# A linear attention product moved next to the probabilities' product, and its query transposes put into the run of the other transposes

## The reference, cut to what matters

```
def causal_linear_attn(q, k, v):                 # BUCKET = 64, e = 32
    q = softmax(q, axis=-1);  k = elu(k) + 1.0
    bq, bk, bv = (z.reshape(b, h, n // BUCKET, BUCKET, e) for z in (q, k, v))
    k_cum = cumsum(bk.sum(axis=-2), axis=-2)
    ctx = cumsum(einsum('bhund,bhune->bhude', bk, bv), axis=2)
    ctx = ctx / (k_cum[..., None] + 1e-06)
    ctx = pad(ctx, one bucket in front)[:, :, :-1]
    return einsum('bhund,bhude->bhune', bq, ctx).reshape(b, h, n, e)

def local_attn(q, k, v):                         # window 128, looks one window back
    dots = where(causal or padding, -max, einsum(q, k2) * e ** -0.5)
    return einsum(softmax(dots), v2)

for i in range(DEPTH):                           # 4 layers, dim 256, 8 heads of 32
    x = x + self_attention(layer_norm(x), Wq, Wk, Wv, Wo, bo)   # local heads, then linear heads, @ Wo
    x = x + gelu(layer_norm(x) @ W1 + b1) @ W2 + b2
```

## Time and profile before

| | us |
|---|---|
| three executions | 957.61, 958.55, 958.65 |
| the profiled execution, its own time | 958.88 |
| its span, first to last instruction | 957.0 |
| PE busy / PEld busy | 944.3 (99%) / 815.4 |
| DVE / ACT / POOL busy | 672.8 (70%) / 612.4 (64%) / 480.0 (50%) |

### The profile page before, as it was taken

How to read it: one execution, slowest core, us unless ns; L and a number is a source line. 1 busy time by engine, 2 the same in 40 slices (tenths; PEclk the granted TensorE clock), 3 DMA queues, 4 the chain that set the end, 5 groups by cost and what they waited for, 6 DMA issues and landing times.

```text
span 957.0 us, 21341 instructions
## 1 busy us (share of the span) xinstructions
PE 944.3 (99%) x8394; PEld 815.4 (85%) x8394; DVE 672.8 (70%) x1531; ACT 612.4 (64%) x1387; POOL 480.0 (50%) x381
## 2 busy tenths in 40 slices
PE   7999999999999999999999999999999999999998
PEld 4687888888888889888888888888997889998997
DVE  7696868677677868696777668776662676766445
ACT  3777777786867867777778676786856345444220
POOL 3437365456836472776466366816247224006453
PEclk9999999999999999999999999999999999999999
DMA  6221000001110000021000002000028597720001
GB/s 211 88 91 45 2 17 2 4 15 51 40 45 18 2 1 18 1 89 45 8 11 2 18 2 82 6 2 7 2 57 203 135 203 147 177 50 1 23 23 45
DMA packets 71582, 47.56 MB, mean 50 GB/s; under 512 B 44511, under 2 KB 68159, under 8 KB 71487
## 3 DMA queue, kind: packets, MB, share of 16 engines
q1 hardware_dynamic: 71487, 46.27, 18.6%
HBM read 44.16 MB, written 2.10 MB: 48 GB/s over the span
## 4 chain that ended last, share of the span: by engine, by line
PE 94%; DVE 4%; ACT 1%; issue 1%; DMA 1%; POOL 0%; SPq 0%; POOLq 0%; DVEq 0%; ACTq 0%
PE F L1464 21%; PE F L1618 19%; PE A L1464 16%; PE A L1805 5%; PE A L1798 5%; PE A L1563 4%; PE A L1958 4%; PE A L1521 3%; PE A L1580 2%; PE A L1478 2%; PE F L1478 2%; PE F L1457 2%; PE A L1554 1%; PE A L1457 1%; PE A L1537 1%; PE A L1674 1%
## 5 line engine op out<-in xcount | busy, mean ns | idle before, releaser
L1464 PE MATMUL F<-xt,w 128*128 128x512 f32 x864 | 217.8, 400 | 0.2 <-ACT scratch L1221 0.2
L475 POOL TENSOR_TENSOR ht<-scratch,ht 128x512 fp32r<-128x512 f32 x128 | 176.0, 1396 | 29.4 <-ACT ht L1224 27.9
L1464 PEld LDWEIGHTS F<-xt,w 128*128 128x128 f32 x864 | 157.6, 188 | 38.2 <-issue 3.0
L1618 PE MATMUL F<-w,ht 128*128 128x256 f32 x1536 | 188.8, 282 | 0.0
L1618 PEld LDWEIGHTS F<-w,ht 128*128 128x128 f32 x1536 | 182.8, 188 | 5.3 <-issue 4.6
L463 POOL TENSOR_TENSOR rstd<-var,minus_half 128x4 f32<-128x4 f32 x32 | 37.6, 1174 | 178.8 <-DVE var L611 178.1
L1221 ACT ACTIVATE scratch<-F,b_now 128x512 f32<-128x512 f32 x128 | 87.7, 685 | 36.6 <-POOL ht L475 19.1
L1464 PE MATMUL A<-wa,xt 128*128 128x512 f32 x372 | 89.8, 397 | 0.0
L470 POOL TENSOR_TENSOR x<-x,vec_f 128x1024 f32<-128x1024 f32 x16 | 38.0, 2376 | 94.0 <-DVE scratch L631 94.0
L1224 ACT ACTIVATE ht<-scratch 128x512 fp32r<-128x512 f32 x128 | 81.1, 634 | 4.0
L1464 PEld LDWEIGHTS A<-wa,xt 128*128 128x128 f32 x372 | 69.0, 188 | 15.9 <-issue 0.2
(11 more groups left out here) (264 smaller groups left out, 2040.3 us busy)
## 6 DMA issues: line engine op xcount, KB each, us to landing
raw_f<-in_L_attn_W_dram SPq DMA_DIRECT2D x8, 1024.0 KB, 5.5
scratch<-in_L_ffn_fc_B_dram SPq DMA_DIRECT2D x32, 256.0 KB, 4.4
scratch<-in_L_ffn_fc_A_dram SPq DMA_DIRECT2D x32, 256.0 KB, 3.9
raw_f<-in_L_ffn_fc_A_dram SPq DMA_DIRECT2D x32, 64.0 KB, 3.2
scratch<-in_x_dram SPq DMA_DIRECT2D x1, 2048.0 KB, 11.0
raw_f<-in_L_ffn_fc_B_dram SPq DMA_DIRECT2D x32, 64.0 KB, 3.2
x<-in_x_dram SPq DMA_DIRECT2D x3, 512.0 KB, 3.7
out_dram<-x SPq DMA_DIRECT2D x3, 512.0 KB, 2.9
```

What stands on the lines that cost most here:

```text
L475: pool.tensor_tensor(ht[:, 1, m, :], hf[:, m % 2, :], ht[:, 0, m, :].bitcast(F32), ALU.subtract).then_inc(h_lo, 1)
L1464: last = pe.matmul(out, lhs(a, c), rhs(b, c), start=clear and k == 0, stop=k == len(total) - 1, skip_group_check=not clear)
L1618: last = pe.matmul(F[:, t % 2, 0:D], ht[:, a, c, P * t:P * t + P], w2[:, b, c, :], start=k == 0, stop=k == len(passes) - 1)
```

## The change

For n of 2 and more (the functions choose the bank by n, the steps of groups 0 and 1 keep their order):

- TensorE: `pe_qnt` moves from before `pe_s` of the second half to behind the fourth tile of `pe_y`, directly in front of `pe_xt`, and TensorE waits for `ctxn_done` in front of it, since the transposed queries go to the bank that `dve_ctx` reads. `pe_lin` moves from the middle of `pe_xt` to directly in front of `pe_pv`; it writes bank 0 instead of bank 1 (`lin_bank`) and waits for `pnorm_out`, which frees that bank. `pe_pv` no longer waits for `lin_lo`.
- The wait for `qnt_out` moves from `pe_ctx` to `pe_pnorm`; that for `kf_done` goes from `pe_qnt` into `pe_ctx`.
- ScalarE: `act_qnt` moves from in front of the second exponentials to behind `act_pt` of the first half; `act_lin_hi` moves from in front of `act_pspread` to behind `act_al_hi`.
- VectorE: `dve_lin_lo` moves from in front of `dve_pt` of the first half to behind `dve_al_lo`.

No instruction is added or removed, and no transfer is moved.

```diff
@@ lin_bank, dve_lin_lo
+        def lin_bank(n):
+            return A[:, 1 if n < 2 else 0, :]
...
-            lo(dve, later_buckets(at[:, 1, 1, :]), later_buckets(A[:, 1, :]),
+            lo(dve, later_buckets(at[:, 1, 1, :]), later_buckets(lin_bank(n)),
                later_buckets(at[:, 0, 1, :])).then_inc(lin_lo, 1)
@@ step of VectorE
                 if attn:
-                    dve_lin_lo(dve, n)
                     dve_pt(dve, n, 0)
...
                 if attn:
                     dve_al_lo(dve, n)
+                    dve_lin_lo(dve, n)
@@ step of ScalarE
                     act_exp(act, n, 0)
                     act_seed(act, n, 1)
-                    act_qnt(act, n)
                     act_exp(act, n, 1)
...
                 act_xt_hi(act, 1, n - 1)
                 if attn:
-                    act_lin_hi(act, n)
                     act_pspread(act, n)
                     act_pt(act, n, 0)
+                    act_qnt(act, n)
...
                 if attn:
                     act_al_hi(act, n)
+                    act_lin_hi(act, n)
                 gelu(5)
@@ functions of TensorE
         def pe_qnt(pe, n):
-            pe.wait_ge(kf_done, n + 1)
             pe.wait_ge(qn_done, n + 1)
@@ pe_ctx
+            pe.wait_ge(kf_done, n + 1)
             for b in range(2):
@@ pe_lin
-                        last = pe.matmul(A[r, 1, cols], ctxn[r, b, u - 1, 0:E], qnt[r, cols], start=True, stop=True)
+                        last = pe.matmul(lin_bank(n)[r, cols], ctxn[r, b, u - 1, 0:E], qnt[r, cols], start=True, stop=True)
@@ pe_pv
-            pe.wait_ge(lin_lo, n + 1)
+            if n < 2:
+                pe.wait_ge(lin_lo, n + 1)
@@ step of TensorE
                     y(2)
-                    pe_qnt(pe, n)
                     pe_s(pe, n, 1)
-                    pe.wait_ge(qnt_out, n + 1)
                     pe_ctx(pe, n)
                     y(3)
+                    pe.wait_ge(ctxn_done, n + 1)
+                    pe_qnt(pe, n)
...
                 pe_xt(pe, 1, n - 1, (0,))
-                if attn:
-                    pe.wait_ge(ctxn_done, n + 1)
-                    pe_lin(pe, n)
-                else:
+                if not attn:
...
                 h(0, 1)
                 if attn:
+                    pe.wait_ge(qnt_out, n + 1)
                     pe_pnorm(pe, n)
                     pe_pt(pe, n, 1)
                 h(2, 3)
                 if attn:
+                    pe.wait_ge(pnorm_out, n + 1)
+                    pe_lin(pe, n)
                     pe_pv(pe, n)
```

More of the change, by code:

```diff
@@ L1184, in act_lin_hi @@
             act.wait_ge(lin_psum, n + 1)
-            act.activation(later_buckets(at[:, 0, 1, :]), later_buckets(A[:, 1, :]), ACT.Copy).then_inc(lin_hi, 1)
+            act.activation(later_buckets(at[:, 0, 1, :]), later_buckets(lin_bank(n)), ACT.Copy).then_inc(lin_hi, 1)
         def act_exp(act, n, b):
```

## The result

The changed kernel takes 960.33 us (median of 9 runs, 959.56 to 962.17); beside it on the same chip the kernel before took 958.61 us (9 runs, 957.61 to 959.26). The ratio is 1.0019, with an interval of 1.0011 to 1.0028: slower by 1.7 us. The forecast was 959.3. The profiled execution took 960.12 us against 958.88.

A forecast was written before the change was run, and what follows sets the result against it. TensorE, busy 99% of the span, was taken as the bound. A saving of 14 x 0.15 us against 2.8 us of new waits gave +0.7 us, 959.3 us from 958.55, with an 8 in 10 range of 957.0 to 961.2.

The forecast's parts named there:

- the third rival: `pe_qk` waits 0.14 us in each of seven early-arrival steps, 1.0 us more, 960.3; with `act_qnt` uncovered 962.4; chance 0.16.
- The stream is shorter by 0.15 a step: TensorE's instructions, through `pe_lin`'s new place: 0.15 us saved per step (0.07 to 0.25), 2.1 us over 14 steps.
- The query transposes move for nothing: `pe_qnt` costs TensorE the same 0.44 us at either place, sum nothing; the scores come 0.44 us earlier.
- `pe_pt` waits for the exponentials in six steps: TensorE at `pe_pt`: waits of 0.53 us in n = 5, 9, 13 and 0.23 in n = 3, 7, 11.
- `pe_h` waits 0.07 in the eight early steps: TensorE waits 0.07 us for VectorE's `xt_lo` in n = 2, 4, 6, 8, 10, 12, 14, 15.
- `act_lin_hi` in the chain to `pe_qk` costs nothing (0.01): End of step: 0.37 us added against slack of 0.31, with 0.05 coming back; 0.01 a step, counted as nothing.
- Step 15 counted with the early ones, -0.08: The last step was put among the eight early steps, each forecast to change by -0.08 us.
- `lin_lo` behind `al_lo` is covered: VectorE's `lin_lo` ends at 216.3, before `pe_wo` at 216.86: covered by 0.4 us, keeping its 0.55.
- the rival that it would be slowed beside GpSimd: `lin_lo` takes 1.29 us beside GpSimd, delaying `pe_wo` 0.4 a step, 5.6 us more, 964.9; chance 0.06.

The follow-up runs named there:

- e4: Changed kernel with `pe_lin` one product earlier, between two groups of `pe_h`, so that it stands alone: 962.54 us, ratio 1.0040.
- e3: Changed kernel with the query transposes and `act_qnt` back at their old places, so only `pe_lin` moves on TensorE: 962.83 us, ratio 1.0048.
- e7: e3 with two query transposes repeated as a filler between `pe_y` and `pe_xt`: 963.18 us, ratio 1.0045.
- e2: Changed kernel with VectorE's minima of the second half ahead of the third residual addition: 957.84 us, ratio 0.9995.
- e8: Kernel before the change, with only the minima moved ahead of the third residual addition: 958.5 us, ratio 0.9996.
- e6: e5 with the second residual addition also ahead of the layer norm's work on VectorE: 959.0 us, ratio 1.0003.
- e1: Changed kernel with ScalarE's `act_lin_hi` one Gelu earlier, out of the chain to `pe_qk`: 959.06 us, ratio 1.0003.
- e5: Changed kernel with the edits of e1 and e2 together: 957.31 us, ratio 0.9983.

## Why the prediction came out as it did

The time was right within 1.0 us and on the right side of no change, and the main mechanism is there: the stream got shorter, and TensorE gave more than that back at the exponentials of six steps. Part of the closeness is luck, since errors in both directions stand in the sum. It is luck too that the third rival's number, 960.3, is the measured one: it has 0.14 us at `pe_qk` in seven steps, where the runs show 0.06 in thirteen.

- *The stream is shorter by 0.15 a step.* Right. In n = 4 `pe_pv` starts 0.157 us earlier in its step than before. By the earlier trace rows, 0.09 of it stood in front of the old `pe_lin` (0.53 for four transposes of 0.44) and 0.06 behind it (0.50 for the next four). e4 gives the price of a lone group between products of 512 columns (0.20; the bounds were 0.07 to 0.25).
- *The query transposes move for nothing.* Right for the stream, but it missed what else they do: at the new place they cover the last residual addition, 0.30 in each of eleven steps (e3, e7). The prediction took 1.83 - 0.96 for `pe_xt` alone, and never asked for whom `pe_xt` waits. Had the change been `pe_lin`'s move alone, the same reasoning would have been wrong by 4 to 5 us, as e3's expectation was.
- *`pe_pt` waits for the exponentials in six steps.* Right in place, engine and steps: e2 takes 0.32 to 0.36 from n = 5, 9, 13 and 0.18 to 0.21 from n = 3, 7, 11, and the same edit takes nothing in the kernel before (e8). The late start of TensorE behind a result was mis-sized: 0.15 was taken, VectorE's case; behind the last exponential TensorE starts 0.05 later, 0.02 behind VectorE. That makes the waits 0.43 and 0.14 for the forecast 0.53 and 0.23. But another cost was not in the sum: where a wait is met, or met only just, the next weights have not been loaded ahead, and twelve transposes take 1.53 in place of 1.47 us. In n = 5, 9, 13 the fourth tile of `pe_y` also comes 0.16 late behind the residual addition; that wait takes the place of a part of the one at `pe_pt` and adds nothing, as e6 shows. The steps came out at +0.44 for +0.38 and +0.12 for +0.08.
- *`pe_h` waits 0.07 in the eight early steps.* Too much: the start of `pe_h` moved by 0.952 us in its step, all of the 0.95. Not the 0.15 was off here but `xt_lo`. VectorE in n = 4 after:

```profile
196.45 1.29 DVE L635 TENSOR_TENSOR xt<-F,xt 128x512 fp32r<-128x512 f32 x2 [0.62 <-ACT xt L1147]
```

  The first half ends at 196.45 + 0.69 = 197.14 and `pe_h` starts at 197.29, 0.15 later; this distance is 0.145 or 0.146 us in each of the 14 steps after. Before it was 0.55 to 1.03. But `xt_lo` ends 0.06 earlier in the step than the prediction let it, since ScalarE's `xt_hi`, which followed the exponentials without a gap before (0.64 us), starts 0.03 earlier and takes 0.60. So `pe_h` stands right at this limit in every step: an even shorter stream ahead of it would bring nothing unless `xt_lo` came earlier too.
- *`act_lin_hi` in the chain to `pe_qk` costs nothing (0.01).* This is the step that failed. It cost some 0.06 in the first product of `pe_qk`, in 13 steps (e1: 2.79 to 2.85 us). Of the 0.37 added more came back than the 0.05 counted, since ScalarE starts the copy of the local result 0.20 earlier in the step; `xt_lo` ends only 0.16 later. But the prediction measured the slack to the start of the product, 0.31, and the weight load runs ahead of it: before, it stood at 213.84, only 0.24 behind the end of `xt_lo`'s first half (213.60). In the seven even steps this error and the one at `pe_h` nearly cancel: -0.5 us for the forecast -0.56.
- *Step 15 counted with the early ones, -0.08.* Wrong, it has +0.23. There the same `act_lin_hi` pushes a Gelu on which TensorE waits:

```profile
700.16 0.47 ACT L1188 ACTIVATE at<-A 128x384 fp32r<-128x384 f32 x1
700.53 0.68 ACT L1224 ACTIVATE scratch<-F,b_now 128x512 f32<-128x512 f32 x1
...
696.67 6.25 PE L1467 MATMUL F<-xt,w 128*128 128x512 f32 x24
702.76 0.51 PE L1467 MATMUL A<-wo,at 128*128 128x256 f32 x3
```

  These are ScalarE and TensorE of the kernel after (L1188 `act_lin_hi`, L1224 the Gelu). In this step the eight transposes of `pe_xt` for the next group's projection, 0.79 us, do not stand among the 24 products of `pe_h`, so TensorE reaches the last six of them sooner and waits for the bank that this Gelu frees at 701.21. The 24 products take 702.76 - 696.67 = 6.09 us; before they took 5.71. With e1 the step takes 40.58 us, 0.15 less than before: the saving and nothing else. Of the 0.7 us between forecast and measured sum this one step is 0.31. The prediction had read n = 4, 5 and 3, and not the last step, which has another order of work.
- *`lin_lo` behind `al_lo` is covered.* Right; the rival that it would be slowed beside GpSimd did not come. The kernel after, VectorE and GpSimd in n = 4:

```profile
212.77 1.29 DVE L635 TENSOR_TENSOR xt<-A,xt 128x512 fp32r<-128x512 f32 x2 [3.83 <-ACT xt L1147]
213.97 0.68 DVE L635 TENSOR_TENSOR at<-scratch,at 128x512 fp32r<-128x512 f32 x1
214.54 2.55 POOL L475 TENSOR_TENSOR ht<-scratch,ht 128x512 fp32r<-128x512 f32 x2 [0.92 <-ACT ht L1227]
214.57 0.55 DVE L635 TENSOR_TENSOR at<-A,at 128x384 fp32r<-128x384 f32 x1
```

  `lin_lo` (128x384) lasts 0.55 with GpSimd at work beside it, and the rule of the Trainium skill that the prediction drew on, SBUF — State Buffer, section Who interferes with whom, agrees with it. `al_lo`, with both inputs in SBUF, took 1.29 and takes 0.68 here, where GpSimd starts only at 214.54: that too agrees, and came as a gain that I hadn't counted. `lin_lo` ends at 215.1 and not at 216.3.

What stays open: 0.24 us that the late steps keep over the even ones in e5. The rows say where: `pe_pt` starts 0.05 behind the last exponential in n = 5 of e5 and of e6, and the minima ahead of the exponentials start without idle time on VectorE. So VectorE is late by its own work, and e6 shows that the residual additions' order is not the cause. Whether it is VectorE's slower work while the weights of a new layer are split wasn't tried.

## What to carry to other kernels

When a piece of work is taken out of a full engine's stream, ask of the instructions behind it what they wait for: the piece may be the cover of a wait that no view of before shows, and the saving is then lost unless something else takes its place. A change that makes the leading engine faster spends slack at each of its waits; list the slack at all of them, in the late steps and in the last one too, measured to the weight load and not to the product behind it, and count a slack near zero as a cost (0.06 us here), not as nothing. Where the followers are late, reorder them (here two edits of a few lines) before the change is given up.

## What the hardware showed that was not expected

- A wait that is met only just costs TensorE more than its idle time: 0.06 us in `pe_qk`, and 1.53 for 1.47 us in `pe_pt`. The rows of its products in the view of waits don't show it. It shows in the length of the group behind, and where the wait is a little longer in the rows of the weight loads (4.4 us in 15 waits for 1.5 in 2).
- The 24 products of `pe_wo` (fp32r, 256 columns) run at one of two rates, 2.74 or 2.83 us for all of them, a whole step at one rate. The slower came in the even steps of e1 from n = 4 on, in n = 12 and 14 of e4, in n = 2 before, in n = 10 after, in one step of e5 and three of e6, at a granted clock of 1.00. What chooses is open; in e1's profiled execution it hid 7 x 0.09 = 0.6 us of the gain.
- TensorE's product started 0.145 or 0.146 us after VectorE's `xt_lo` in front of `pe_h` in all 14 steps after (0.15 in the earlier trace rows), and 0.05 after ScalarE's last exponential (six steps). One latency for all pairs of engines isn't what these rows show.
